# Moving three quarters of the output and FFN epilogue in between the attention heads of the last query slot

## The reference, cut to what matters

```python
def reference(x, W_qkv, W_o, ternary_weight, bias, act_scale):   # x: (4, 4096, 1024) float32
    x = _layernorm(x + attn(x, W_qkv, W_o))       # 16 heads of 64, RoPE on Q and K, causal softmax
    x = _layernorm(x + ffn(x, ternary_weight, bias, act_scale))
    return x

def ffn(x, ternary_weight, bias, act_scale):
    scale = jnp.maximum(act_scale, 1e-05)
    x_int = jnp.clip(jnp.round(x / scale), -127., 127.)
    w = ternary_weight.astype(jnp.float32) - 1.0
    return jnp.einsum('bsi,oi->bso', x_int * scale, w) + bias
```

## Time and profile before

| | |
|---|---|
| median of 3 runs | 1754.79 us (1749.77 to 1755.55) |
| the profiled execution's own time | 1752.02 us |
| its span on the slowest core | 1750.4 us |
| spans of the eight cores | 1739.2 to 1750.4 us |
| busy: TensorE, ScalarE, VectorE | 66%, 56%, 34% |
| phase 1 | to about 618 us |
| attention (phase 2) | about 618 to 1453 us |
| epilogue (phase 3) | about 1453 us to the end |

### The profile page before, as it was taken

One profiled execution on the slowest core, in us unless ns is written; L12 is line 12 of the kernel. 1 busy time (PEld: TensorE's weight loads), 2 busy tenths in 40 slices (PEclk: granted clock), 3 DMA queues, 4 the chain that ended last, 5 costly groups with the idle time before them and its releaser, 6 DMA issues.

```text
span 1750.4 us, 18404 instructions; the slowest of 8 cores (1739.2 to 1750.4 us)
## 1 busy us (share of the span) xinstructions
PE 1147.4 (66%) x5064; PEld 379.3 (22%) x5064; DVE 597.0 (34%) x1177; ACT 974.6 (56%) x1195; POOL 30.6 (2%) x55
## 2 busy tenths in 40 slices
PE   1001788888876726776777878788888885565564
PEld 0001333333332201111111111112222221222221
DVE  0002233333433315533333232322312123666664
ACT  0002333333334426678888888889889994444543
POOL 0001000000000000000000000000000000000000
PEclk9999999999999957689999998999999997787877
DMA  9993644455543162232233131322232001121211
GB/s 98 117 171 99 120 103 117 110 117 126 120 97 78 41 122 65 83 110 79 79 115 111 61 112 60 131 95 76 80 146 76 1 1 48 49 66 55 72 49 48
DMA packets 112818, 153.30 MB, mean 88 GB/s; under 512 B 38736, under 2 KB 93008, under 8 KB 108368
## 3 DMA queue, kind: packets, MB, share of 16 engines
q1 hardware_dynamic: 65536, 113.26, 19.6%
q0 software_dynamic: 13648, 30.48, 12.1%
q10 hardware_dynamic: 33536, 8.39, 2.9%
HBM read 132.26 MB, written 46.14 MB: 102 GB/s over the span
## 4 chain that ended last, share of the span: by engine, by line
PE 42%; ACT 23%; DVE 11%; issue 11%; DMA 5%; another core or an unknown queue 4%; ACTq 3%; DVEq 0%; POOL 0%; POOLq 0%; SPq 0%
ACT exp_b L484 16%; PE pAV L506 9%; PE pC L364 6%; DVE exp_b L495 5%; PE pSC L469 5%; PE pA L312 4%; PE pR L612 4%; PE pB L312 4%; PE pR L699 3%; ACT kraw L318 3%; ACT recb L515 2%; DMA maskb<-masks 2%; ACTq L240 1%; DMA w_sti<-tern 1%
## 5 line engine op out<-in xcount | busy, mean ns | idle before, releaser
L484 ACT ACTIVATE exp_b<-pSC 128x1024 bf16<-128x1024 f32 x640 | 606.3, 1052 | 143.3 <-PE pSC L474 133.1
L506 PE MATMUL pAV<-exp_b,v_run 128*128 128x512 bf16 x1280 | 416.0, 410 | 91.9 <-DVE exp_b L495 91.1
L495 DVE TENSOR_TENSOR exp_b<-exp_b,maskb 128x512 bf16<-128x512 bf16 x512 | 211.8, 425 | 365.5 <-ACT exp_b L484 307.0
L469 PE MATMUL pSC<-q_run,k_run 64*128 64x512 bf16 x640 | 252.8, 404 | 114.8 <-ACT exp_b L484 101.8
L474 PE MATMUL pSC<-q_run,k_run 64*128 64x512 bf16 x640 | 258.0, 412 | 0.0
L469 PEld LDWEIGHTS pSC<-q_run,k_run 64*128 64x128 bf16 x640 | 57.4, 94 | 413.0 <-issue 413.0
L506 PEld LDWEIGHTS pAV<-exp_b,v_run 128*128 128x128 bf16 x1280 | 77.2, 98 | 273.8 <-issue 273.8
L364 PE MATMUL pC<-w_kvT,x_T 128*128 128x512 bf16 x512 | 115.7, 379 | 0.0
L318 ACT CAST kraw<-pA 128x512 bf16<-128x512 f32 x48 | 28.1, 586 | 153.3 <-PE pA L312 145.5
L267 PE MATMUL pD<-identb,w_st 128*128 128x128 bf16 x32 | 4.0, 305 | 139.2 <-DVE w_st L261 139.2
L522 DVE TENSOR_TENSOR attn_n<-pAV,recb 64x512 bf16<-64x512 f32 x32 | 21.8, 683 | 211.9 <-ACT recb L518 210.6
(11 more groups left out here) (103 smaller groups left out, 989.5 us busy)
## 6 DMA issues: line engine op xcount, KB each, us to landing
v_scr<-v_stg SPq DMA_DIRECT2D x32, 512.0 KB, 3.8
v_run<-v_scr SPq DMA_DIRECT2D x8, 2048.0 KB, 7.9
v_run<-v_scr SPq DMA_DIRECT2D x8, 1536.0 KB, 6.7
x_tm<-x_kv POOLq DMA_DIRECT2D x8, 1024.0 KB, 10.9
k_scr<-krot SPq DMA_DIRECT2D x64, 128.0 KB, 2.6
v_run<-v_scr SPq DMA_DIRECT2D x8, 1024.0 KB, 5.2
k_run<-k_scr SPq DMA_DIRECT2D x8, 1024.0 KB, 4.8
xo<-x_own SPq DMA_DIRECT2D x16, 512.0 KB, 4.3
```

Of the source, the lines that this page charges most:

```text
L469: s.add("T", (lambda sb_, bi, t: lambda te: te.matmul(pSC[sb_][:, 0:512], k_run[bi][0:64, t * 128:(t + 1) * 128], q_run[bi][0:64, :], star ...
L484: s.add("SC", (lambda eb, sb_: lambda sc: sc.activation(exp_b[eb][:, :], pSC[sb_][:, :], ACTF.Exp))(eb, sb_), reads=[f"pSC{sb_}"], writes= ...
L495: s.add("V", (lambda eb, moff, half: lambda v: v.tensor_tensor(exp_b[eb][:, half * 512:(half + 1) * 512], exp_b[eb][:, half * 512:(half + ...
L506: s.add("T", (lambda eb, bi, t, hh, n, pit: lambda te: te.matmul(pAV[pit][:, hh * 512:(hh + 1) * 512], v_run[bi][:, t * 256 + hh * 128: t ...
```

## The change

1. The epilogue is emitted inside phase 2. After each head of slot 3 (`sl == 3`) 8 rounds of the epilogue of blocks 0 to 11 (the rows of slots 0 to 2) are emitted, before the next head. After the last head is normalised, blocks 12 to 15 follow, 28 rounds. The separate phase 3 is gone.
2. In slot 3 the scores use `pSC[0]` only; `pSC[1]` is the accumulator of both epilogue matmul stages. There are no `pR` and no `pT` any more.
3. Stage 8 is 8 DMA transposes of 128x128, issued by ScalarE, in place of 8 TensorE transposes and a copy.
4. Buffers: `k_run`, `v_run`, `q_run` two instead of three; `maskb` half as large and loaded anew for each slot; `xo`, `ylnf`, `uf`, `uf2`, `rdl`, `xq_bf`, `xq_T` two instead of four, `ui32` one; the second norm writes its result to `xo`, which is stored. `bias_bc`, which nothing read, is gone with its two matmuls.
5. In a round the blocks are emitted newest first (`reversed`).

```diff
-        bias_bc = sb("bias_bc", [128, D], F32)
...
-            maskb = sbp("maskb", [128, 2 * 8 * 512], BF16)
-            k_run = [sbp(f"k_run{i}", [128, 4096], BF16) for i in range(3)]
+            maskb = sbp("maskb", [128, 8 * 512], BF16)
+            k_run = [sbp(f"k_run{i}", [128, 4096], BF16) for i in range(2)]
...
+                elif st == 8:
+                    for c in range(8):
+                        s.add("SC", (lambda c, bi: lambda e: e.dma_start_transpose(
+                            xq_T[bi % 2][:, c * 128:(c + 1) * 128],
+                            xq_bf[bi % 2][:, c * 128:(c + 1) * 128]))(c, bi),
+                            reads=[f"xq_bf{bi % 2}"], writes=[f"xq_T{bi % 2}"], dma=True)
...
-                bi = it % 3
+                bi = it % 2
+                if j == 0:
+                    mdst = maskb[:].rearrange("p (b c) -> p b c", b=8)
+                    msrc = masks[sl % 2, :, :, :].rearrange("b p c -> p b c")
+                    s.add("G", (lambda mdst, msrc: lambda g: g.dma_start(
+                        out=mdst, in_=msrc))(mdst, msrc), writes=["maskb"])
...
-                    sb_ = t % 2
+                    sb_ = (t % 2) if sl < 3 else 0
...
+                if sl == 3:
+                    target = (j + 1) * 8
+                    while ep_k_holder[0] < target:
+                        for g16 in reversed(range(12)):
+                            st = ep_k_holder[0] - OFF * g16
+                            if 0 <= st < NSTAGE:
+                                emit_stage(g16, st)
+                        ep_k_holder[0] += 1
+
+            for k in range(ep_k_holder[0], NSTAGE + OFF * 11 + 1):
+                for g16 in reversed(range(12)):
...
             if pending_tail is not None:
                 emit_tail(*pending_tail)
                 pending_tail = None
+            for k in range(NSTAGE + OFF * 3 + 1):
+                for g16 in reversed(range(12, 16)):
+                    st = k - OFF * (g16 - 12)
+                    if 0 <= st < NSTAGE:
+                        emit_stage(g16, st)
```

More of the change, by code:

```diff
@@ L212, in build_nc @@
                   reads=["bias_row", "sc_sb"], writes=["biasb"])
[L213 to L219, removed]
             s.add("T", lambda t: t.matmul(pB[:, 0:1], ones_f[0:1, 0:128], sc_sb[0:1, 1:2],
@@ L225, in build_nc @@
                   reads=["ones_f", "sc_sb"], writes=["pB"])
-            s.add("V", lambda v: v.tensor_copy(bias_bc[:], pA[:, :]),
-                  reads=["pA"], writes=["bias_bc"])
             s.add("V", lambda v: v.tensor_copy(sprime_bc[:], pB[:, 0:1]),
@@ L434, in build_nc @@
             psp = lambda name, shape, dt: ph.enter_context(nc.psum_tensor(name, shape, dt))
-            maskb = sbp("maskb", [128, 2 * 8 * 512], BF16)
-            k_run = [sbp(f"k_run{i}", [128, 4096], BF16) for i in range(3)]
-            v_run = [sbp(f"v_run{i}", [128, NKT * 256], BF16) for i in range(3)]
-            q_run = [sbp(f"q_run{i}", [128, 512], BF16) for i in range(3)]
+            maskb = sbp("maskb", [128, 8 * 512], BF16)
+            k_run = [sbp(f"k_run{i}", [128, 4096], BF16) for i in range(2)]
+            v_run = [sbp(f"v_run{i}", [128, NKT * 256], BF16) for i in range(2)]
+            q_run = [sbp(f"q_run{i}", [128, 512], BF16) for i in range(2)]
             exp_b = [sbp(f"exp_b{i}", [128, 1024], BF16) for i in range(3)]
@@ L442, in build_nc @@
             pAV = [psp(f"pAV{i}", [128, 1024], F32) for i in range(2)]
-            s = Sched(CH, KS)
[L445 to L448, removed]
+            ND = 4
+            xo = [sbp(f"xo{i}", [128, 1024], F32) for i in range(2)]
+            y1f = [sbp(f"y1f{i}", [128, 1024], F32) for i in range(ND)]
@@ new lines, in build_nc @@
+            ylnf = [sbp(f"ylnf{i}", [128, 1024], F32) for i in range(2)]
+            uf = [sbp(f"uf{i}", [128, 1024], F32) for i in range(2)]
+            uf2 = [sbp(f"uf2{i}", [128, 1024], F32) for i in range(2)]
+            ui32 = [sbp("ui32", [128, 1024], I32)] * 2
+            rdl = [sbp(f"rdl{i}", [128, 1024], F32) for i in range(2)]
+            sqb = [sbp("sqb0", [128, 1024], F32)] * 2
+            xq_bf = [sbp(f"xq_bf{i}", [128, 1024], BF16) for i in range(2)]
+            xq_T = [sbp(f"xq_T{i}", [128, 1024], BF16) for i in range(2)]
@@ L450, in build_nc @@
+            NSTAGE, OFF = 16, 4
+            ep_k_holder = [0]
             iters = [(sl, j) for sl in range(NSLOT) for j in range(NPAIR)]
@@ L492, in emit_mask @@
                     w = t - (n - 8)
-                    moff = ((sl % 2) * 8 + w) * 512
+                    moff = w * 512
                     for half in range(2):
@@ L545, in build_nc @@
                 pending_tail = (sl, j, it % 2)
+                if sl == 3:
[8 more added lines that the diff above has]
+                for g16 in reversed(range(12)):
+                    st = k - OFF * g16
+                    if 0 <= st < NSTAGE:
+                        emit_stage(g16, st)
             if pending_tail is not None:
@@ L767, in build_nc @@
             s.run(block, bar)
+            bar = barrier_counts()
             @block.sync
```

359 lines of the change are left out of this document (150 added, 209 removed).

## The result

| | before | after |
|---|---|---|
| median | 1752.99 us (10 runs) | 2262.73 us (9 runs) |
| ratio | | 1.290, 95% interval 1.289 to 1.292 |
| spans of the cores | 1739.2 to 1750.4 us | 2224.6 to 2255.1 us |
| mean granted clock | 0.916 to 0.921 | 0.786 to 0.818 |

The change makes the kernel 29% slower; 2308 was predicted. Some executions show one die at a lower clock and take some per cent longer (one of the ten before, 1779.7 us): they count in the medians, but not in the ratios and in what is worked out from a ratio.

What follows compares the result with a forecast made beforehand. Bounds: ScalarE's exps in slot 3, an epilogue loop through TensorE and VectorE with no engine full. Slot 3's start 1151.8, heads 489.6, gaps 19 + 468.6, attention's end 8.9, four blocks 168.4, plus 1.6: 2308 us, range 2100 to 2460.

Steps and rivals of the forecast that it cites:

- eight heads: Slot 3's heads with one score buffer: 61.2 us each, 489.6 us in all.
- six gaps: Exposed epilogue rounds and loads after heads 1 to 6 of slot 3: 78.1 us each, 468.6 us.
- four blocks at the end: Epilogue of the last four blocks after attention: 21.5, three loops 109.8 and 37.1, together 168.4 us.
- One score buffer: Slot 3's scores and exps wait for each other: steps of 1.74 to 1.96 us, taken as 1.87.
- Pieces: Eight DMA transposes a block wait on one name, uncovered: 2.76 us each, 22.1 us a block.
- Moving: Epilogue between slot 3's heads stays exposed by program order; only projection matmuls hide; a block's loop 36.6 us, against 17.08.
- Loads: Next head's k, v and q in slot 3, issued only after the last store: 10.6 us a gap.
- Mask and buffers: Half mask load saves 13 us, slot 1's reload returns some 3: -10; two k/v/q buffers covered in slots 0 to 2.
- Pieces cheap: Rival, chance 0.07: a block's DMA transposes overlap, eight costing about 6 us; 2050 us in all.
- pieces dear: Rival, chance 0.09: each DMA transpose in the epilogue costs 4.97 us; 2590 us in all.
- One buffer cheap: Rival, chance 0.05: slot 3's steps stay at 0.92 to 1.1 us, about 200 us less, 2108 us.
- The rival on the other side: Faster, chance 0.02: work between slot 3's heads vanishes into the steps' idle time; 1742 us, or 1709 with 1.74 us steps.

Runs made afterwards that it cites:

- e9: Kernel before with two score buffers, TensorE transposes, early loads and the epilogue of blocks 0 to 11 in portions between slot 3's heads: 1756.62 us, ratio 0.999.
- e3: Changed kernel with the next head's loads in slot 3 issued before the epilogue rounds, not after them: 2185.5 us, ratio 1.245.
- e4: Changed kernel with all epilogue rounds of blocks 0 to 11 after the last head instead of between heads: 2226.91 us, ratio 1.268.
- e5: Kernel before with only the mask buffer halved and loaded anew for each slot: 1757.54 us, ratio 1.0015.
- e6: Kernel before with only stage 8 done by 8 DMA transposes of one name, in its own phase 3: 1993.39 us, ratio 1.135.
- e2: Kernel before with only one score buffer in slot 3: 1959.62 us, ratio 1.115.
- e8: Two score buffers, TensorE transposes, early loads, epilogue of blocks 0 to 11 in portions inside slot 3's steps: 1681.85 us, ratio 0.958 to the kernel before.
- e1: Changed kernel with a name of its own for each of a block's 8 transposed pieces: 2143.62 us, ratio 1.222.

## Why the prediction was right

Step by step, predicted against the trace of the changed kernel (core 6):

| term | predicted | measured |
|---|---|---|
| start of slot 3 | 1151.8 | 1146.9 |
| eight heads | 489.6 | 474.0 |
| first gap | 19 | 17.1 |
| six gaps | 468.6 | 454.2 |
| last exp to projection | 8.9 | 6.3 |
| four blocks at the end | 168.4 | 156.6 |
| span | 2306.3 | 2255.1 |

The mechanism was right in its three main terms, and each term came out below its forecast, so the 45 us over are sizes and not errors that cancelled; only within the gaps two of them did.

- **One score buffer.** The chain was read correctly, 0.57 + 1.17 from a head's beginning. The steps are 1.67 us (1.73 with masks) at the full clock and 1.88 at the lower, not 1.74 and 1.96. The mixture of clocks assumed from slot 0 fits: 147 of 240 steps, 61%, ran at the lower clock, where 58% was assumed. Alone it costs 202 us.
- **Pieces.** 2.42 us each (19.35/8) against 2.76, so 128 x 0.34 = 44 us too much. Gaps and end together came out only 28 us shorter: the loads took more (below), and so did the FFN matmuls, 6.3 and 6.9 us to the residual's start in the gap shown, not 5.7. The price was also split otherwise than assumed: scaling the issue with the rows was wrong. It is 1.11 us for 128 rows and was 1.27 for 1024 in the earlier trace rows, and the landing after it is 1.2, not 2.5. Alone the pieces cost 237 us. The Trainium skill's fixed cost of about 2.0 us per DMA (DMA: Bandwidth & Descriptors, Anatomy of one DMA) is given for the GpSimd path; these pieces, issued by ScalarE, took 2.3 us to landing, between that figure and my 2.69.
- **Moving.** Program order exposes the work between heads, as said: e9 has two score buffers, TensorE transposes and early loads, and still gains nothing. That moving hides only the projection was too strict: with the loads out of the way, e3 is 41 us faster than e4.
- **Loads.** 77 us shown by e3, 13 of them a gap; predicted 10.6 a gap. I took the row of a `v_run` whose `k_run` was issued 3 us before it. Issued together they take 11.1 us in the median, and from the store of stage 15 to the first score it is 12.3 to 14.7 us in the six gaps.
- **Mask and buffers.** The table's first row sets core 6 beside a term built on core 0 (1161.8), and cores differ by up to 13 us there. Over all eight cores the first mask multiplication starts 12.6 us earlier in the mean (630.4 against 643.0; 13 predicted) and slot 3's first exp 14.7 us earlier (1140.7 against 1155.4; 10 predicted): the 3 us that the reload was to cost do not show, nor do the two K/V/Q buffers cost anything in slots 0 to 2. In e5, the mask part alone, slot 3 begins only 4.6 us earlier. Why the two differ was not tested; e5 keeps three K/V/Q buffers and so has more loads at the start.
- **Sum of parts.** 1756 + 202 (one buffer) + 237 (pieces) + 77 (loads) = 2272, against 2263 measured. That this fits so well is partly luck, for it leaves out three things. The rest of the smaller epilogue costs more: 33.8 us a block in e4 against 31.8 in e6, so some 32 in all. The earlier start saves some 15 and interleaving 41.

**The rivals.** Pieces cheap and pieces dear both missed by a price that lay between. One buffer cheap fell with e2. The rival on the other side asked for what is exposed between heads to be under a few us a gap; it was 76. No run here tests its best case, 1742 us with one score buffer. The nearest is e8, with two: it hides the work and pays for it, 154 us more in slot 3 (441 against 287) for 214 less at the end (88 against 302), and comes out 74 us better than before.

## What to carry to other kernels

Emitting work between two loops of an in-order engine moves it and hides little of it (nothing that shows in e9, some 41 us of e3); to overlap it, put it into the steps in portions no larger than the slack of each engine, ordered so that each result is asked for some steps later. Before taking a buffer from a loop for that, read at a loop's beginning what a step takes without overlap. And count as one chain all DMAs that write one tracked name, and everything queued behind them.

## What the runs showed of the hardware

- A stretch in which TensorE never idles longer than 1.7 us can still run mostly at the lower clock: in e2 it ran one score pair and two pAV matmuls per 1.7 to 1.9 us step, and the granted clock was 0.63 over 493 us. Two more 512-column matmuls a step brought it to 0.96, and the kernel became some 30 us faster by doing more.
- A DMA transpose of 128x128 from SBUF costs ScalarE's queue 1.11 us to issue, nearly the 1.27 us of one with eight times the rows from DRAM; eight in a row took 10.30 us to issue (e1). It lands 2.3 us after the issue starts.
